# One chain scanned at a time, sixteen tokens a step, in a fused state-space and attention kernel

## What is computed

```python
xr, gate = split(x @ W_in.T, 2);  xr = xr + cond          # 512 channels each
xc = silu(conv4(xr) + b_conv)                             # depthwise, causal
xn = layernorm(xc) * ln_g + ln_b
Bm, Cm, dt = split(xn @ W_xproj.T, 3)                     # 16 states each
Ad = 1 + tanh(dt @ W_dt.T + b_dt) * 0.01 * (-tanh(A_log))
Bd = Bm * minimum(norm(xn), 1)
for t in range(64):                                       # per sequence
    h  = clip(h * Ad[t][:, None] + Bd[t][:, None] * xn[t][None, :], -10, 10)
    ys[t] = Cm[t] @ h                                     # h is 16 x 512
x = x + ((ys + D * xn) * silu(gate)) @ W_out.T
```

## Time and profile before

| | us |
|---|---|
| median of 3 runs (lowest, highest) | 1804.61 (1801.22, 1805.07) |
| the profiled execution | 1796.04 |
| its span, first to last instruction | 1794.1 |
| PE busy | 1610.8 (90%) |
| PE weight loads | 1042.8 (58%) |
| DVE busy | 1341.5 (75%) |
| POOL busy | 1226.3 (68%) |
| ACT busy | 1160.8 (65%) |

### The profile page before, as it was taken

How to read it: one execution, slowest core, us unless ns; L and a number is a source line. 1 busy time by engine, 2 the same in 40 slices (tenths; PEclk the granted TensorE clock), 3 DMA queues, 4 the chain that set the end, 5 groups by cost and what they waited for, 6 DMA issues and landing times. The chain is left out here.

```text
span 1794.1 us, 41468 instructions
## 1 busy us (share of the span) xinstructions
PE 1610.8 (90%) x12460; PEld 1042.8 (58%) x12460; DVE 1341.5 (75%) x2306; ACT 1160.8 (65%) x2921; POOL 1226.3 (68%) x1874
## 2 busy tenths in 40 slices
PE   5345877799999999999999999999999999999886
PEld 4233333356666666666666666666666655555664
DVE  1423577788888888888888888888888888876442
ACT  3555554567777777777777777777777753444453
POOL 1587766787888887878787887888787873233231
PEclk8657777999999999999999999999999999999998
DMA  4013445565566556565655565556666564533220
GB/s 106 16 54 69 107 105 127 140 147 147 147 148 148 142 131 171 130 167 136 156 147 145 142 149 147 146 144 155 146 149 148 132 163 113 132 89 92 77 66 24
DMA packets 222716, 224.27 MB, mean 125 GB/s; under 512 B 54241, under 2 KB 179553, under 8 KB 222497
## 3 DMA queue, kind: packets, MB, share of 16 engines
q1 hardware_dynamic: 222496, 221.62, 50.8%
HBM read 150.36 MB, written 71.17 MB: 123 GB/s over the span
## 5 line engine op out<-in xcount | busy, mean ns | idle before, releaser
L1635 DVE CUSTOM_DVE_ANT_0 gc<-ps_u,gc,hi 128x512 f32<-128x512 f32 x1008 | 776.4, 803 | 56.3 <-PE ps_u L948 37.3
L964 PE MATMUL ps_y<-gc,cms 128*32 128x512 f32 x2048 | 301.5, 622 | 9.0 <-POOL cms L660 7.2
L1256 ACT ACTIVATE a_tap<-a_xr,conv_w 128x128 f32<-128x128 f32 x768 | 245.0, 399 | 14.8 <-DVE a_xr L1567 9.5
L948 PE MATMUL ps_u<-xs_sb,stage 64*128 64x512 bf16 x1024 | 201.3, 433 | 29.4 <-issue 18.4
L538 POOL TENSOR_TENSOR a_tap<-a_tap 128x512 f32<-128x512 f32 x128 | 163.1, 1278 | 65.2 <-ACT a_tap L1256 65.0
L902 PE MATMUL ps<-a_xT,WinT 128*128 128x128 f32 x1024 | 143.4, 300 | 20.6 <-ACT a_bcT L1304 14.7
L902 PEld LDWEIGHTS ps<-a_xT,WinT 128*128 128x128 f32 x1024 | 135.8, 214 | 36.4 <-issue 29.3
L948 PEld LDWEIGHTS ps_u<-xs_sb,stage 64*128 64x128 bf16 x1024 | 75.2, 187 | 103.6 <-issue 70.5
L993 PE MATMUL ps<-WinT,c_xT 128*128 128x512 f32 x256 | 127.3, 620 | 3.7 <-ACT c_xT L1327 3.7
L1031 PEld LDWEIGHTS ps<-c_zT,L1T 128*128 128x128 f32 x1024 | 123.8, 192 | 7.4 <-issue 4.3
L1031 PE MATMUL ps<-c_zT,L1T 128*128 128x128 f32 x1024 | 125.1, 275 | 3.1 <-ACT c_kbd L1377 3.1
(11 more groups left out here) (168 smaller groups left out, 3651.6 us busy)
## 6 DMA issues: line engine op xcount, KB each, us to landing
xs_sb<-xn_parts SPq DMA_DIRECT2D x256, 192.0 KB
xn_parts<-a_parts SPq DMA_DIRECT2D x128, 192.0 KB, 3.0
skip_d_xn<-a_dx SPq DMA_DIRECT2D x64, 256.0 KB, 2.0
xs_sb<-xn_parts SPq DMA_DIRECT2D x128, 128.0 KB
scan_out<-y_sb SPq DMA_DIRECT2D x256, 64.0 KB
c_dx<-skip_d_xn SPq DMA_DIRECT2D x64, 256.0 KB, 3.5
c_y<-scan_out SPq DMA_DIRECT2D x64, 256.0 KB, 3.2
c_wu<-style_rows SPq DMA_DIRECT2D x128, 128.0 KB, 3.4
```

Of the source, the lines that this page charges most:

```text
L948: pe.matmul(ps_u[r][t % 2][:, :], weights[:, :, l * STEPS + t], xs_sb[rows, l % 2, t, :], start=True, stop=True).then_inc(s[f"b_u{r}"], 1)
L964: pe.matmul(ps_y[quad:quad + 32, :], cms[:, slice_no(*chain_of(sig, r)) % 2, v, r, 32 * u:32 * (u + 1)], gc[r][:, (2 * u + v) % RING, :], ...
L1256: ins = act.activation(a_tap[:, tap, m, :].rearrange("p (r t) -> p r t", r=2), a_xr[:, m, :, tap:tap + S], ACT.Identity, bias=bias, scale= ...
L1635: dve._custom_dve(bass.dve_ops.TENSOR_ADD_SAT, out=gc[r][:, t % RING, :], in0=ps_u[r][t % 2][:, :], in1=before, s0=hi[:, c % 4, col:col + ...
```

## The change

One chain is scanned at a time. A scan step covers SPAN = 16 tokens of it; r now means the parity of the token: r = 0 takes the even, r = 1 the odd tokens of the same chain. A chain lasts 4 steps, chains follow each other without overlap, and there are 64 scan steps. The 16 scan operations of a step form one sequence, in which each takes the state that the other r has just written. The weights of a chain are loaded to both halves of the rows. Stage C follows stage A by 13 steps where it was 17, so the program has 81 steps where it had 85, and the kinds of step begin and end elsewhere: second steps are 7 to 12 (before 7 to 16), full steps 13 to 66 (before 17 to 66), late steps 67 to 72 (before 67 to 76). The orders of PE, DVE, ACT and POOL in second, full and late steps are written anew, with other banks. SP's order stays.

```diff
     STEPS = 8
-    SLICES = S // STEPS
+    SPAN = 2 * STEPS
+    SLICES = S // SPAN
...
-    C_LAG = 17
+    C_LAG = 13
     A_DEPTH = 3
     STEP_COUNT = TILES + C_LAG + 4
-    SCAN_STEPS = TPC * CHAINS + TPC
+    SCAN_STEPS = TPC * CHAINS
...
-    def chain_of(sig, r):
-
-        g = sig - TPC * r
-        c = 2 * (g // SLICES) + r
-        return (c, g % SLICES) if g >= 0 and c < CHAINS else None
+    def chain_of(sig):
+
+        return divmod(sig, SLICES) if 0 <= sig < SCAN_STEPS else None
...
             def load_w(c):
...
                 for k in range(SEQS):
-                    sp.dma_start(Wb[r * ROWS + k:(r + 1) * ROWS:SEQS, c // 2 % 2, k, :],
-                                 bdt_dram[c, :, k * DS:(k + 1) * DS, :].rearrange("e d t -> e (d t)"))\
+                    sp.dma_start(Wb[k:2 * ROWS:SEQS, c % 2, k, :],
+                                 bdt_dram[c, :, k * DS:(k + 1) * DS, :].rearrange("e d t -> e (d t)").unsqueeze(0)
+                                 .to_broadcast([2, TERMS, DS * S]))\
                         .then_inc(s[f"b_ld_w{c % 4}"], 16)
...
             def scan_step(sig, t, r):
...
+                c, l = chain_of(sig)
+                q, col = sig * STEPS + t, l * SPAN + 2 * t + r
                 if col == 0:
                     dve.wait_ge(s["b_prep"], PREP * (c + 1))
-                dve.wait_ge(s[f"b_u{r}"], 8 * HEAD + q + 1)
-                dve.wait_ge(s[f"b_g{r}"], HEAD + q)
+                dve.wait_ge(s[f"b_u{r}"], STEPS * HEAD + q + 1)
+                dve.wait_ge(s[f"b_g{1 - r}"], HEAD + q + r)
                 dve.wait_ge(s[f"b_read{r}"], 8 * HEAD + 2 * ((q - RING) // 2 + 1))
-                before = zeros[:, :] if col == 0 else gc[r][:, (t - 1) % RING, :]
+                before = zeros[:, :] if col == 0 else gc[1 - r][:, (t - 1 + r) % RING, :]
```

More of the change, by code:

```diff
@@ L772, in step @@
                 sig, c0 = i - SCAN_LAG, i - C_LAG
-                if chain_due(i, 1) is not None:
-                    split_b(chain_due(i, 1))
                 spread_c(sig)
+                a_second_rest(i - 3)
+                c_bias(c0 - 1)
                 a_var(i - 2)
@@ L778, in step @@
                 a_bias(i - 2)
[L779 to L801, removed]
                 if chain_due(i, 1) is not None:
@@ L805, in late_step @@
                 c_gate_product(c0)
-                c_bias(c0 - 1)
+                a_gain(i - 2)
+                a_shift(i - 2)
+                a_scale_b(i - 3)
+                a_offset(i - 2)
+                a_half(i - 1, 0)
+                a_skip(i - 2)
+                a_half(i - 1, 1)
+                a_sum(i - 1)
+                c_join(c0 - 3)
+                a_norm_root(i - 2)
                 c_style(c0)
-                c_join(c0 - 3)
                 c_var(c0)
                 c_final(c0 - 3)
+                a_first_rest(i - 2)
+                c_root(c0)
+            def late_step(i):
+                sig, c0 = i - SCAN_LAG, i - C_LAG
+                spread_c(sig)
+                c_bias(c0 - 1)
+                if chain_due(i, 1) is not None:
+                    split_b(chain_due(i, 1))
+                c_sum_skip(c0)
+                c_gate_product(c0)
+                c_join(c0 - 3)
+                c_style(c0)
+                c_final(c0 - 3)
+                c_var(c0)
                 c_root(c0)
@@ L1740, in second_step @@
                 sig = i - SCAN_LAG
-                a_take_bc(i - 3, bank[0])
                 a_silu(i - 2)
@@ L1767, in step @@
                 sig, c0 = i - SCAN_LAG, i - C_LAG
+                c_stats(c0 - 1)
+                c_mean_var(c0 - 1)
+                a_take_bc(i - 3, bank[2])
+                scan_step(sig, 0, 0)
                 scan_step(sig, 0, 1)
-                c_stats(c0 - 1)
-                scan_step(sig, 0, 0)
-                a_take_bc(i - 3, bank[0])
+                a_silu(i - 2)
+                scan_step(sig, 1, 0)
+                scan_step(sig, 1, 1)
+                c_silu(c0, bank[0])
+                a_stats(i - 2, bank[1])
@@ L1780, in step @@
-                a_bound_norm(i - 3)
-                a_stats(i - 2, bank[1])
-                a_mean_var(i - 2)
-                scan_step(sig, 2, 1)
-                c_silu(c0, bank[0])
-                scan_step(sig, 2, 0)
-                scan_step(sig, 3, 1)
-                c_demodulate(c0 - 3, bank[2])
-                scan_step(sig, 3, 0)
-                c_scale_q(c0 - 2, bank[0])
-                c_scale_v(c0 - 2, bank[0])
+                scan_step(sig, 3, 0)
+                scan_step(sig, 3, 1)
@@ L1791, in step @@
+                c_scale_q(c0 - 2, bank[2])
+                c_demodulate(c0 - 3, bank[0])
+                scan_step(sig, 4, 0)
+                c_scale_v(c0 - 2, bank[2])
+                a_bound_norm(i - 3)
                 scan_step(sig, 4, 1)
-                scan_step(sig, 4, 0)
+                scan_step(sig, 5, 0)
                 scan_step(sig, 5, 1)
-                scan_step(sig, 5, 0)
-                c_max(c0 - 2, 0, bank[0])
-                c_max(c0 - 2, 1, bank[2])
-                c_subtract(c0 - 2, 0, bank[0])
```

350 lines of the change are left out of this document (167 added, 183 removed).

## The result

The changed kernel takes 1847.21 us (median of 4 runs, 1838.35 to 1852.71), the kernel before 1802.91: 1.0245 times as long, interval 1.0213 to 1.0277. It is slower by 44 us, where 10 us less was forecast, and lies outside the range. The side is that of the last rival, weights that come late.

A forecast was written before the change was run, and what follows sets the result against it. PE was taken to bound the full and late steps. Terms -60.4 (steps), +25 (plain full), +19 (preparing), +6 (second), 0 (late, DMA) gave -10.4 us: 1804.6 to 1794 us, range 1754 to 1822.

The forecast's parts named there:

- the last rival: Weights land late at chain starts: 0.3 us more per load, PE loses 2.4 us at 15 starts, +36, 1830 us; chance 0.27.
- the one under DMA: Weight loads of 32 KB for 16, 16 chains x 8, hide behind the step if landed before the chain's first spread.
- its likeliest case: Plain full steps of 23.5 to 24.0 us, whole kernel 1776 to 1800 us; chance 0.46.
- its point of decision: From 0.7 us lost by PE at each chain start, the change is slower than the kernel before.
- The scan's dependence: On DVE, a scan operation needing its neighbour's result costs 0.2 us (0.93 against 0.72); about +1.2 us per full step.
- The full step: Plain full steps take 23.8 us, +0.6 each; 41 of them give +25 us.
- the two circles: Wait rings in a plain full step: through bank 2, 23.6 us against PE's 23.2; through bank 0, another 0.25.
- The preparing step: Full step that prepares a chain: 25.3 us, +1.45 on 23.89, PE waiting for the gated tile; 13 give +19 us.
- PE stays the bound: First rival: dependences fall into DVE's idle time, full steps keep 23.38 us, -54 in sum, 1750 us; chance 0.27.
- Second steps: Steps with A and scan but no C: 12 dependent neighbours, at most +2.4 us each; +6 us taken over five steps.
- Late steps: Steps with scan and C: added 1.2 us lies in DVE's 2.8 us idle per step, nothing added, cap 6 us.
- structure -60.4: Four one-chain second steps (73.74 us) and four late ones (80.2) go, four full steps (93.5) come: net -60.4 us.

The follow-up runs named there:

- the third experiment: Changed kernel with scan and stage C one step later behind stage A, preparation and weight loads left where they were: 1805.79 us, 1.0032 to the kernel before.
- the second experiment: Changed kernel with each token parity carrying its own state, so neighbouring scan operations don't depend on each other: 1818.78 us, 1.0102 to the kernel before.

## Why the prediction was wrong

*The failed step* is the one under DMA: "It hides behind the step as long as it lands before the chain's first spread", entered in the sum as 0. It doesn't land before. The sum knew of "next to no margin" (25.5 against 25.7), and still priced the doubling at nothing in its likeliest case. The margin itself was read rightly: with half the load PE waits at four chains of the full stage, by 0.3 to 1.5 us. What the doubling put on top is 3 us of landing for each chain.

What that cost in the full stage: eleven of the chains' first steps take 27.04 in the mean, where they take 24.70 with the weights in time; 2.34 x 11 = 26. The thirteenth chain's takes 26.51 against 23.55 in the same program step of the third experiment, 3. At the last chain it is 32.08 against 22.28, also for the same program step, 9.8. Together 39 us, of the 61 that lie between forecast and result (the sum said -10.4, the spans differ by +50.9). The half-load run takes 36.4 of the span back, 3.4 in the second stage, 30.7 in the full and 2.2 in the late one. That the late stage gives back so little of the 9.8 isn't explained in full: in that run PE still waits 2.42 us at the last chain, and the granted clock is 0.88 and 0.81 in the first two late steps (0.94 and 0.79 in the changed kernel).

*The rival* had the mechanism, the place (PE idle ahead of a chain's first spread) and the side, and its point of decision, 0.7 us for each chain, was passed three times over (mean idle 2.2 in the full stage). Its price of 0.3 us a load is what came: from the first issue to the last landing the eight take 8.6 us in the median for 6.1, of which the issue gives 0.5 and the landing takes 3.0. Its 36 us are close to the 39, partly by luck, as the last chain alone makes 9.8. The 17 us between its 1830 and the result lie in other terms. The range ended at 1822, below the price of a rival with a chance of 0.27, so it left out that rival's own time, as it left out the 1750 of the first one.

*The clock behind the idle.* The idle ahead of spreads doesn't turn into time one for one. At the five first steps of the full stage whose granted clock stays at 1.00 (idle 0.70 to 2.37) the step is longer than 24.70 by about 1.0 us less than the idle, or not at all. At the other seven (idle 2.22 to 3.14) the clock of the step is 0.94 four times and 0.88 three times, and the step is 1.4 to 2.8 us longer than that, about 14 us in all. The read-out behind such an idle takes 1.94 us, at the lower of the two levels (1.2 GHz), where the same group took 1.07 at 1018.99. The length of the idle alone doesn't decide: 2.37 left the clock where it was, 2.22 didn't. The last chain's start had 6.94 idle and a clock of 0.79 over its window.

*The scan's dependence* was sized right: 0.22 for 0.21. The prediction set it against the sentence that a semaphore after each operation costs nothing extra (the Trainium skill, VectorE: DVE Perf Modes, The DRAIN you can't avoid). By that rule as the prediction took it the second experiment would change nothing; plain steps went from 23.93 to 23.30. But that experiment keeps a semaphore wait for each operation and leaves out only the wait for the neighbour, so what costs here is the neighbour's result and not the semaphore.

*The full step*: 23.93 for 23.8, +0.73 for +0.6, and 0.54 and 0.17 of it at qv and v, where the two circles were put at 0.4 and 0.25. Over 41 steps 30 us for 25. *The preparing step*: 24.75 for 25.3, but 0.77 is handed to the next step; 1.6 in all for 1.45, 21 us for 19. *PE stays the bound* was refuted mostly by the wait at qv; with another bank there (23.37) it would have been nearly right for plain steps.

*Second steps*: 4 us for 6, by the ledger. That contains two opposite things: PE waits 4.3 us less for weights there (two chain starts for three) and the scan's dependence. They weren't separated. *Late steps*: of the 13.2 that are missing, 9.8 are the last chain's start. In the first late step (26.95 us, before 24.76) PE waits 2.09 us for `c_o` and the granted clock is 0.94; the rest of the remaining 3.4 and the 7.2 at the two ends, for which the sum had nothing, were not traced.

In sum: structure -60.4, plain 30, preparing 21, weights 39, second 4, late 3.4, ends 7.2: +44 against the +50.9 measured. The 7 us left lie in the full stage by the ledger and have no cause shown; 2.7 of them are in its first two steps and go with the half load.

*Left open*: a doubled load in more than two parts, which would tell whether the broadcast's form is the whole of the 3 us.

## What to carry to other kernels

A transfer with a known margin is priced at its landing, from a row with the same bytes and the same form, before anything is called hidden; where either changes, the old number is no bound. A margin of 0.2 us in one place is a term of the sum, multiplied by how often it occurs. When one operation's result becomes its neighbour's input, walk the banks that its engine also frees: here one bank decided whether 0.2 us a pair fell into idle time or into PE's queue, and moving it, with the load a step and the preparation two scan operations sooner, turned 2.5% slower into 2.0% faster.

## What the runs showed of the hardware that wasn't expected

Eight loads of 32 KB, each one source row broadcast to two halves of the partitions, are issued faster than eight of 16 KB (4.20 us against 4.73) and land later, 3.4 to 5.3 us behind the last issue against 1.3 to 1.9. Their semaphores rise in two parts behind the issue where those of the small loads rise in eight. Splitting them doesn't help: 16 loads of 16 KB land 1.3 to 1.9 us behind the last issue, but that comes 9.4 to 10.4 us after the first. And an idle of 2.2 to 3.1 us of PE in a full stage brought a granted clock of 0.94 or 0.88 in that step at seven chains of nine (2.23 and 2.37 left it at 1.00), so that a late transfer costs more than the time it is late.
